# Latent cross-attention block of a two-layer decoder: output projection with four products a unit in place of six

## The reference, cut to what matters

```python
ctx_c   = einsum('bhsl,bld->bhsd', attn, kv_r)          # 256 tokens x 64 latent values for a head
ctx_lat = einsum('bhsd,hkd->bhsk', ctx_c, w_kc_kv)      # w_kc_kv[h]: 128 x 64
ctx     = ctx_lat.transpose(0, 2, 1, 3).reshape(B, S, H * K)
return ctx @ Wo.T                                       # Wo: 256 x 2048
```

## Time and profile before

| | |
|---|---|
| median of 3 runs | 1926.72 us (1924.54 to 1929.82) |
| span of the profiled execution | 1919.4 us; the page gives no other time of it |
| from that span to the median of the runs | 7.3 us |
| PE busy | 1791.9 us (93% of the span), 15752 matmuls |
| DVE, ACT, POOL busy | 67%, 57%, 36% |
| chain that ended last | PE 77%, DVE 11%, ACT 6% |
| latent block | about 779 to 1618 us of the span |

### The profile page before, as it was taken

One profiled execution on the slowest core, in us unless ns is written; L12 is line 12 of the kernel. 1 busy time (PEld: TensorE's weight loads), 2 busy tenths in 40 slices (PEclk: granted clock), 3 DMA queues, 4 the chain that ended last, 5 costly groups with the idle time before them and its releaser, 6 DMA issues.

```text
span 1919.4 us, 42082 instructions
## 1 busy us (share of the span) xinstructions
PE 1791.9 (93%) x15752; PEld 1490.5 (78%) x15752; DVE 1282.1 (67%) x3335; ACT 1088.8 (57%) x2750; POOL 686.3 (36%) x674
## 2 busy tenths in 40 slices
PE   7999998889998998699999999999999998898995
PEld 6999977646656776599999999999999997674663
DVE  5676657742237666488888888888888888775222
ACT  4766654312213333488888888888888885531221
POOL 5643322132223532344433444344433441123221
PEclk8999999989999999899999999999999999999998
DMA  4000019222328000000000000000000001402223
GB/s 165 23 2 1 1 55 359 69 93 45 45 54 266 11 3 2 22 12 12 12 12 12 28 12 12 12 12 12 12 2 12 1 2 72 204 2 81 46 47 66
DMA packets 51861, 91.69 MB, mean 48 GB/s; under 512 B 4592, under 2 KB 43632, under 8 KB 49232
## 3 DMA queue, kind: packets, MB, share of 16 engines
q1 hardware_dynamic: 42928, 78.16, 12.1%
q0 software_dynamic: 8160, 10.29, 3.5%
q10 hardware_dynamic: 576, 0.56, 0.1%
HBM read 56.13 MB, written 32.87 MB: 46 GB/s over the span
## 4 chain that ended last, share of the span: by engine, by line
PE 77%; DVE 11%; ACT 6%; issue 2%; DMA 2%; POOL 2%; SPq 0%; DVEq 0%; ACTq 0%; POOLq 0%
PE bank L100 63%; PE bank L2547 10%; ACT d_PT L1339 2%; ACT landing L1339 2%; PE bank L1160 1%; PE bank L1888 1%; DVE a_t L707 1%; PE bank L505 1%; PE bank L1867 1%; DVE tiny L133 1%; DVE X L172 1%; DVE d_nm L1427 1%; DVE tiny L128 0%; DVE a_t L704 0%; DMA c_sums<-c_y,c_xs 0%
## 5 line engine op out<-in xcount | busy, mean ns | idle before, releaser
L2695 DVE TENSOR_REDUCE e_st<-bank 128x1 f32<-128x496 f32 (+2 forms) x512 | 291.6, 570 | 122.1 <-PE bank L100 121.0
L2632 ACT ACTIVATE e_P<-bank,e_st 128x496 f32<-128x496 f32 (+2 forms) x512 | 307.2, 600 | 94.5 <-DVE e_st L2699 92.9
L2714 DVE TENSOR_TENSOR e_PT_lo<-bank,e_PT_hi 128x512 fp32r<-128x512 f32 (+1 forms) x448 | 287.2, 641 | 1.5 <-ACT e_PT_hi L2647 1.4
L2547 PE MATMUL bank<-ident,e_P 128*128 128x128 f32 (+1 forms) x1664 | 258.3, 274 | 4.2 <-DVE e_PT_lo L2714 3.7
L2647 ACT CAST e_PT_hi<-bank 128x512 fp32r<-128x512 f32 (+1 forms) x448 | 248.5, 555 | 10.7 <-PE bank L2547 6.6
L100 PE MATMUL bank<-e_PT_hi,e_kv 128*128 128x256 f32 (+1 forms) x832 | 249.0, 320 | 0.0
L2547 PEld LDWEIGHTS bank<-ident,e_P 128*128 128x128 f32 (+1 forms) x1664 | 194.9, 140 | 31.0 <-issue 26.3
L100 PE MATMUL bank<-e_PT_lo,e_kv 128*128 128x256 f32 (+1 forms) x832 | 215.6, 279 | 0.0
L100 PE MATMUL bank<-e_KT,e_qk_hi 128*128 128x496 f32 (+2 forms) x512 | 199.0, 389 | 7.2 <-ACT e_P L2632 5.7
L100 PE MATMUL bank<-e_KT,e_qk_lo 128*128 128x496 f32 (+2 forms) x512 | 177.1, 346 | 0.0
L100 PEld LDWEIGHTS bank<-e_PT_lo,e_kv 128*128 128x128 f32 (+1 forms) x832 | 158.4, 190 | 2.4
(11 more groups left out here) (470 smaller groups left out, 4955.9 us busy)
## 6 DMA issues: line engine op xcount, KB each, us to landing
c_wall<-in_c_w SPq DMA_DIRECT2D x8, 1536.0 KB, 18.9
g_wall<-in_g_w SPq DMA_DIRECT2D x8, 1536.0 KB, 19.1
c_rows<-normed SPq DMA_DIRECT2D x9, 1040.0 KB, 12.8
g_rows<-normed SPq DMA_DIRECT2D x9, 1040.0 KB, 13.5
e_stage<-in_e_w SPq DMA_DIRECT2D x16, 416.0 KB, 3.2
c_xs<-c_rows SPq DMA_DIRECT2D x23, 130.0 KB, 2.1
g_xs<-g_rows SPq DMA_DIRECT2D x23, 130.0 KB, 2.1
landing<-in_a_wo SPq DMA_DIRECT2D x2, 1024.0 KB, 6.0
```

Source lines behind the costliest of these rows:

```text
L2547: last = pe.transpose(o[0:rows, c * SEQ + i * P:c * SEQ + (i + 1) * P], p[:, i, k0:k0 + rows], ident[:])
L2632: act.activation(Pm[u % 2][:, i, STARTS[j]:STARTS[j] + n], bank[score_bank[j]][:, 0:n], ACT.Exp, bias=s[:, i, 4:5], accum_out=s[:, i, j:j ...
L2695: last = dve.tensor_reduce(s[:, i, j:j + 1], bank[score_bank[j]][:, 0:PIECES[j]], AX.X, ALU.max)
L2714: dve.tensor_tensor(lo, bank[tb_bank[at % 2]][0:rows, 0:n * SEQ].rearrange("p (c n) -> p c n", c=n), hi.bitcast(F32), ALU.subtract).then_i ...
```

## The change

The folded weight's upper buffer is as before. Its lower buffer becomes a stacked one: the upper part of W_h on partitions 0 to 63 (a second ACT copy) and the lower part on partitions 64 to 127 (DVE, on these 64 partitions alone). The context's lower buffer is stacked too: its lower part on partitions 0 to 63 (DVE, 64 partitions), and on partitions 64 to 127 a copy of the upper part of partitions 0 to 63, which a second ACT copy writes from PSUM partitions 0 to 63. The projection is then upper buffer x upper buffer plus stacked x stacked: two products for each 128 tokens, four a unit.

```diff
             def upper_o(self, h, o):
                 act.wait_ge(*self.o_folded.at(h + 1))
-                act.copy(self.wf[h % 2][0][:], o[:, 0:D]).then_inc(*self.wf_hi.up())
+                act.copy(self.wf[h % 2][0][:], o[:, 0:D])
+                act.copy(self.wf[h % 2][1][0:LAT], o[0:LAT, 0:D]).then_inc(*self.wf_hi.up())
...
             def lower_o(self, h, o):
-                dve.tensor_tensor(lo[:], o[:, 0:D], hi[:].bitcast(F32), ALU.subtract).then_inc(*self.wf_lo.up())
+                dve.tensor_tensor(lo[LAT:P], o[LAT:P, 0:D], hi[LAT:P].bitcast(F32), ALU.subtract).then_inc(*self.wf_lo.up())
...
                     def project_out(u):
...
-                            last = mm3(o[:, i * D:(i + 1) * D], (c[0][:, rows], c[1][:, rows]), [x[:] for x in wf[h % 2]],
-                                       True, True)
+                            for n in range(2):
+                                last = mm(o[:, i * D:(i + 1) * D], c[n][:, rows], wf[h % 2][n][:], n == 0, n == 1)
...
                     def keep_context(u):
-                        act.copy(cx[u % 2][0][:], bank[ctx_bank][:, 0:SEQ]).then_inc(*cx_hi.up())
+                        act.copy(cx[u % 2][0][:], bank[ctx_bank][:, 0:SEQ])
+                        act.copy(cx[u % 2][1][LAT:P], bank[ctx_bank][0:LAT, 0:SEQ]).then_inc(*cx_hi.up())
...
                     def lower_context(u):
-                        dve.tensor_tensor(cx[u % 2][1][:], bank[ctx_bank][:, 0:SEQ], cx[u % 2][0][:].bitcast(F32),
+                        dve.tensor_tensor(cx[u % 2][1][0:LAT], bank[ctx_bank][0:LAT, 0:SEQ], cx[u % 2][0][0:LAT].bitcast(F32),
                                           ALU.subtract).then_inc(*cx_lo.up())
```

## The result

The changed kernel took 1940.0 us (median of 4 runs, 1936.2 to 1942.1), the kernel before 1927.6 (4 runs, 1924.5 to 1929.8): slower by 0.6%, ratio 1.0062 with a 95% interval of 1.0044 to 1.0079. The forecast was 1941.1.

What follows compares the result with a forecast made beforehand. The prediction took the chain score, maximum, exponential, score to bound step 0, not PE's work. Held ACT copies +10.4, the fold +4.4 and the products -0.4 made +14.4 us, so 1941.1 us; range 1925 to 1944.

Steps and rivals of the forecast that it cites:

- The products are worth nothing: project_out: two fewer products take 15.1 us off PE, but it waits longer for the exponential; gain only 0.4 us.
- the block's end: With no scores left, up to two products may be on the chain; half the bound taken, -0.4 us.
- PE's wait in step 0: Step 0 of each turn, before the score: the wait for ACT's exponential grows from 0.26 to 0.50 us.
- ACT is held in step 2: Case 1: copy into partition 64 and upper_qk start late, upper_pt 0.17 us a unit late, +10.4 us; chance 0.50.
- The fold: Once a head: held ACT copies delay the exponential 0.51 us, the chain 0.29 us; 15 heads, +4.4 us.
- the smaller alternative: Fold without ACT holds: DVE's lower_o and the next instruction held, last maximum 0.15 us late, 2.3 us over 15 heads.
- The sum: Over the profiled span of 1919.4 us: +10.4 + 4.4 - 0.4 = +14.4 us, giving 1941.1 us.
- The base: Profiled span 1919.4 us; the 7.3 us up to the median 1926.7 taken as lying around it, unchanged.
- Case 2: ACT's copies in step 2 overlap as ever; +2.3 - 0.4 = +1.9 us, so 1928.6 us; chance 0.37.
- Case 3: PE's work in the latent block is the bound; -15.1 us, so 1911.6 us; chance 0.08.
- Case 4: Copy longer than 0.37 us, or lower_context late too; each 0.05 us a unit 3 us, 1945 to 1950; chance 0.05.

Runs made afterwards that it cites:

- four_only: Kernel before with project_out cut to four products a unit, the upper x lower terms left out, no copy added; 1923.95 us, ratio 0.9995, block 792.0 us.
- copy_across: Kernel before plus one unread ACT copy in step 2, from partitions 0-63 to 64-127; 1933.7 us, ratio 1.0047, block 802.9 us.
- copy_straight: Kernel before plus one unread ACT copy in step 2, from partitions 0-63 to 0-63; 1926.2 us, ratio 1.0003, block 792.8 us.
- restacked: Changed kernel with stacked halves exchanged: ACT's copies start on partition 0, DVE's lower_context writes 64-127, lower_o on 0-63; 1936.85 us, ratio 1.006, block 801.5 us.
- fold_straight: Changed kernel with DVE's lower_o over all 128 partitions as before, overwriting the copied upper weight; 1937.0 us, ratio 1.0054, block 803.6 us.
- pooled: Changed kernel with GpSimd making both upper copies, ACT as before, lower_o on all partitions; 1923.99 us, ratio to the kernel before 0.9995, block 792.0 us.
- reordered: Kernel before, six products, with ACT's bank 3 exponential, PE's step 7 score moved earlier and DVE's last lower_pt later; 1904.18 us, ratio 0.9888, block 777.2 us.

## Why the prediction was right

**The products are worth nothing.** Right, and shown: four_only gains 0.8 us of 15.1, of which the prediction had 0.4 for the block's end. PE's wait in step 0 grew from 0.26 to 0.50, as predicted.

**ACT is held in step 2.** Right, and this was the step on which forecast and second case parted, at 0.50 against 0.37. It was carried over from DVE's rows, with no row of ACT for it. Starts at +0, +0.39, +0.78, +1.05 as predicted; copy_across costs 10.1 us of a predicted 10.4. That it is the change of start partition and not the copy is shown by copy_straight (0.0) and restacked.

**The fold.** The size was nearly right (predicted 4.4 us, 0.29 a head; measured 3.8, or 5.3 if the 1.5 us left over below are the fold's), the step was not. The prediction said that with holds the ACT instructions behind the copy are 0.51 late and hand this on through PE's score. Its own rule excluded that: the fold's copy goes from partition 0 to partition 0, so nothing was to be held on ACT, and nothing was; the exponential is only 0.25 late. What the prediction had as the smaller alternative, DVE's hold at 0.15, measures 0.11 + 0.08 + 0.09 = 0.28, as there is a third held instruction that it did not count: the lower_pt behind the maximum. That maximum reads PSUM only, so the lower_pt is the first to read SBUF from partition 0 after lower_o read it from 64. That this is why it is held fits restacked, where lower_context only writes from 64: there two instructions are held, and the next lower_pt keeps its 0.58 us behind the maximum. fold_straight takes all three away and gets back 3.8 us. Two errors of opposite sign met, and that the fold came out near its price is luck. The range did not depend on it: by the prediction's own alternative, 2.3 us, the sum is 1939.0.

**The sum.** ACT's holds +10.1, DVE's +3.8 and the products -0.8 make 13.1 of the 14.6 measured. The remaining 1.5 us are 0.1 a head; the fold's second ACT copy, which makes its exponential 0.25 us late, is the likely place, but no run took it away alone. It is not lower_context on half the partitions, since pooled has that and is as short as four_only. Over the four turns of one head the distances between the first products of project_out add up to 50.8 us before and 51.8 after, +0.99, where the prediction's terms make 4 x 0.17 + 0.29 = 0.97.

**The base.** The prediction put 7.3 us around the span. The profiled execution after took 1942.1 us with a span of 1940.9, which leaves 1.2. The profiled execution before was thus most likely one quicker than its median, as its clock of 0.979 suggests (0.974 in the one after), and not one with 7 us around it. Taking the difference in the block onto the median, which is what the sum amounted to, was the right way nevertheless.

**The rivals.** Case 2 (ACT overlaps as ever) is what copy_straight shows: right for a copy that stays on its partitions. Case 3 (PE bounds) is refuted twice, most plainly by reordered: with all of PE's work in place the block lost 15.6 us, about what case 3 had hoped for from removing 15.1 us of it. Case 4 did not come: the copy took 0.36 us.

The Trainium skill (VectorE: DVE Perf Modes, section "Two Vector instructions with no wait between them") keeps its rule on quadrants to VectorE. On DVE the trace agrees (0.71, 0.46 and 0.69 us against 0.60, 0.38 and 0.60), the third instruction included, since the rule counts each memory by itself. On ACT the runs go beyond it: its instructions are held in the same way, at 0.39 against 0.26 us.

## What to carry to other kernels

A copy that an engine with slack takes on can be free by its duration and still cost, if it starts on another partition than its neighbours: count the instruction behind it as held too, and put such copies on an engine that is not in the chain. Before removing work from the busiest engine, look for its short regular waits and at what ends them; while that chain stands, the removed time comes back as a longer wait, and three moved calls gave here what two fewer products of six did not. Read the size of a small change from the distance between two marks around the stage, as the whole run scatters by more than it.

## What the runs showed of the hardware that was not expected

- ACT instructions that start on another partition than the one ahead do not overlap it. A 64x256 or 128x256 copy of 0.37 us is followed after 0.39 instead of 0.26, both going and coming back, and for a change on the read side alone as well as on the write side. Only starts at 0 and 64 were tried.
- On DVE a hold costs 0.08 to 0.12 us on these shapes. Behind lower_o, which reads and writes from 64, it was seen on the lower_pt behind the maximum too, with that instruction, which reads no SBUF, in between; behind restacked's lower_context, which only writes from 64, it was not.
- GpSimd's copies across partitions cost the block nothing (792.0 with and without them).
